# V by Strassen products in a gated cross-attention and FFN block: seven products per pair of key tiles for contexts 1 to 7

## The chip, the cores and the metric

The kernel runs on one core of a Trainium2 chip. The metric is the device time of one execution in microseconds (us), with the span and the granted TensorE clock of the core beside it. In the profile, PE is the TensorE matmul, PEld its weight load, DVE is VectorE, ACT is ScalarE, POOL is GpSimd and SP is SyncE, which here only issues DMAs.

## The reference, cut to what matters

Eight sequences of 1024 rows attend, each with a causal mask, to a context of their own, and a feed-forward network with ternary weights follows. Every product must come out near float32, so the kernel runs each as three float16 passes (see below).

```
x, ctx: (8, 1024, 512); w_q, w_k, w_v: (512, 512); W1: (2048, 512); W2: (512, 2048)

q = layernorm(x) @ w_q;  k = ctx @ w_k;  v = ctx @ w_v
attn = softmax(causal(q @ k.T / sqrt(512)))
x = x + tanh(g_xattn) * (attn @ v)
h = gelu(layernorm(x) @ ternary(W1).T + b1)
x = x + tanh(g_ffn) * (h @ ternary(W2).T + b2)

ternary(w) = clip(round(w / mean|w|), -1, 1)
```

## The kernel before, in words

There are 64 tiles of 128 rows, eight to a context ("batch" in the code). The kernel is written by hand, engine by engine: each engine has its own function `slot`, called once for every tile t, and the order of its lines is the order of that engine's queue. Cross-engine order is by semaphores, and each engine takes its instructions strictly in turn. In what follows, i is t mod 8, the tile's place in its context.

An operand in float32 is split into an upper and a lower float16 half. ACT writes the upper half (`*_upper`), DVE the lower one (`*_lower`), and PE multiplies in three passes (`PASSES`): upper by upper, lower by upper, upper by lower.

In slot t, PE does in this order: the scores of tile t against the (i+1) key tiles of its context, 12 matmuls per 512 keys or rest (L1319); `t_product` for tile t+2, the normalised rows times the product of w_q and w_k, 24 matmuls of 256 columns (L1281); `v_product`, V of key tile t+1, 12 matmuls of 512 columns (L1300); and attn times V of tile t-1, called PV below, 3 matmuls of 512 columns for each key tile up to that tile's own (L1349). Scores of tile t+1 reuse the PSUM of those of tile t.

DVE in slot t: the mask, the row maximum and the bias of the softmax (L909 to L915), statistics of x of tile t+5 (L920), the lower half of the attention weights (L929), `t_lower` (L873), `ln_rows` (L850), `v_lower` (L880), and the output rows of tile t-1 (L956 to L963, "the o update"), which wait for PV. Some slots add a part of the next context: two halves of its maximum (L821), its scale, and `ctx_lower`, the lower half of 256 context columns (L756). In 16 slots a `ternary` step makes 1024 columns of W1 or W2 into -1, 0, 1 (L1091, L1093).

ACT in slot t: the exponential (L573) and the upper half of the weights (L578), `t_upper` (L588), `rows_upper` (L596), `ctx_upper` (L563), `v_upper` (L601). POOL in slot t is short: a power (L446) and the lower half of the normalised rows (L450). SP loads, stores and turns rows by transposing DMAs; it waits in its queue for the o update of every tile before the tile's store (L368).

The raw context of 2 MB lies in `raw`, one context at a time. The float16 weights W1 and W2 lie in `w1_s` and `w2_s`.

The FFN follows. It multiplies the normalised rows by W1 by Strassen's seven products already, in 32 units of 4 hidden tiles (L1198), and then by W2 (`back`, L1254). Its first rows are prepared inside the last attention slots: from tile FIRST_Y = 57 on, each slot normalises one tile (`y_stats`, `y_normal` on DVE), POOL forms sums (`y_sums`, L477 to L482), ACT and POOL split them (`y_upper` L641, `y_lower` L488) and SP turns them (`turn_y`, L334). `weight_sums` (L1004) makes four sums of W1 halves on DVE, two in slot 62 and two in slot 63. PE runs the first three products of unit 0 after the scores of slot 63 (`unit_first`) and goes on after the PV of slot 62 (`unit_second`, which waits for all weight sums).

## Time and profile before

| | us |
|---|---|
| median of 3 runs | 1590.83 (1590.52 to 1591.98) |
| the profiled execution | 1590.56 |
| its span in the trace | 1588.7 |
| granted clock of TensorE, mean | 0.997 |
| PE busy | 1567.5 (99%) |
| DVE busy | 1094.7 (69%) |
| ACT busy | 811.6 (51%) |
| POOL busy | 481.6 (30%) |

A busy PE is the union of modelled matmul intervals, in which the end of one covers the start of the next. How densely PE really works is seen better from the starts in the timeline: a group of n matmuls takes the time to the start of the group behind it. The chain of work that ended last is 95% PE.

### The profile page before, as it was taken

To read this page: it belongs to the slowest core of one execution; us is meant where nothing else is said; L and a number is where in the kernel's file an instruction comes from. 1 tells how busy PE (TensorE), PEld (TensorE's weight loads), DVE (VectorE), ACT (ScalarE), POOL (GpSimd) and SP (SyncE) were. 2 spreads that over 40 slices of the span, in tenths; PEclk is the share of its full clock that TensorE was granted. 3 is DMA by queue.
4 is the path that set the end of the run, shared out by engine and by line. 5 is a ranking of instruction groups with operands and counts; after the bars stand their busy time and mean duration, and the time that the engine had idled before them with its cause. 6 is when DMAs were issued, how large, how long until landed. Compare 5 with 4: busy or idle time off the path is not lost.

```text
span 1588.7 us, 26066 instructions
## 1 busy us (share of the span) xinstructions
PE 1567.5 (99%) x10024; PEld 979.6 (62%) x10024; DVE 1094.7 (69%) x1824; ACT 811.6 (51%) x1448; POOL 481.6 (30%) x468
## 2 busy tenths in 40 slices
PE   7899999999999999999999999999999999999998
PEld 4556555565656565564666666666666666666665
DVE  7766656577787777766567667766776676767654
ACT  2334444433332333333666666666666666666654
POOL 4311111111111111134144444444433453345330
PEclk9999999999999999999999999999999999999999
DMA  8547667654656655553322242233332332324110
GB/s 212 130 103 192 149 182 153 175 137 121 165 128 163 141 160 145 129 123 78 81 77 77 47 100 77 77 67 80 81 87 68 66 98 79 77 47 100 51 51 27
DMA packets 307964, 170.81 MB, mean 108 GB/s; under 512 B 268208, under 2 KB 268224, under 8 KB 306688
## 3 DMA queue, kind: packets, MB, share of 16 engines
q1 hardware_dynamic: 306368, 166.52, 43.0%
q10 hardware_dynamic: 1296, 2.36, 0.4%
q8 instruction: 79, 1.29, 0.3%
q14 instruction: 45, 0.37, 0.1%
q0 software_dynamic: 176, 0.27, 0.1%
HBM read 70.53 MB, written 33.55 MB: 66 GB/s over the span
## 4 chain that ended last, share of the span: by engine, by line
PE 95%; DVE 3%; DMA 1%; issue 1%; ACT 0%; SPq 0%; DVEq 0%
PE s_ps L1254 14%; PE e_ps L1254 14%; PE s_ps L1319 11%; PE o_ps L1349 11%; PE v_ps L1300 10%; PE t_ps L1281 10%; PE t_ps L1198 7%; PE o_ps L1198 7%; PE v_ps L1198 7%; PE m_ps L1198 3%; DMA ctx_s<-in_wqT 1%; DMA raw<-in_ctxT 0%; DVE cmax L821 0%; DVE wv_s L1004 0%; PE e_ps L1349 0%
## 5 line engine op out<-in xcount | busy, mean ns | idle before, releaser
L1056 DVE SCALAR_TENSOR_TENSOR v_s<-xnT,sc,v_s 128x512 f16<-128x512 f32 x256 | 239.0, 954 | 106.3 <-ACT v_s L681 106.3
L674 ACT ACTIVATE xnT<-tT,b_s 128x256 f32<-128x256 f32 x384 | 174.0, 500 | 182.9 <-DVE tT L1050 66.6
L1254 PE MATMUL s_ps<-w_s,v_s 128*128 128x512 f16 x1024 | 262.8, 379 | 0.0
L1254 PE MATMUL e_ps<-w_s,v_s 128*128 128x512 f16 x1024 | 262.8, 379 | 0.0
L573 ACT ACTIVATE p<-s_ps,ebias,esc 128x128 f32<-128x128 f32 (+3 forms) x64 | 53.2, 831 | 339.3 <-DVE ebias L915 339.3
L1319 PE MATMUL s_ps<-ctx_s,tT 128*128 128x512 f16 (+3 forms) x1152 | 197.7, 326 | 3.2 <-DVE tT L873 3.2
L1349 PE MATMUL o_ps<-v_s,pT 128*128 128x512 f16 x840 | 191.6, 379 | 0.1
L681 ACT ACTIVATE v_s<-xnT,sc 128x512 f16<-128x512 f32 x256 | 176.3, 712 | 7.5
L1300 PE MATMUL v_ps<-wv_s,ctx_s 128*128 128x512 f16 x768 | 176.5, 379 | 1.2 <-DVE v_s L880 0.8
L1254 PEld LDWEIGHTS e_ps<-w_s,v_s 128*128 128x128 f16 x1024 | 100.2, 98 | 120.8
L1281 PE MATMUL t_ps<-xnT,a_s 128*128 128x256 f16 x1488 | 172.7, 273 | 0.5 <-ACT a_s L649 0.5
L1319 PEld LDWEIGHTS s_ps<-ctx_s,tT 128*128 128x128 f16 x1152 | 105.8, 98 | 95.1 <-DVE tT L873 4.1
L1281 PEld LDWEIGHTS t_ps<-xnT,a_s 128*128 128x128 f16 x1488 | 144.8, 98 | 22.8 <-issue 0.9
L501 POOL TENSOR_TENSOR tT<-tT 128x512 f32<-128x512 f32 x64 | 81.5, 1273 | 245.7 <-ACT tT L701 245.7
L446 POOL TENSOR_TENSOR rstd<-var_s,minus_half 128x1 f32<-128x1 f32 x61 | 34.0, 557 | 382.8 <-DVE var_s L844 382.8
L1349 PEld LDWEIGHTS o_ps<-v_s,pT 128*128 128x128 f16 x840 | 82.1, 98 | 97.2 <-DMA pT<-p_s 0.6
L1254 PEld LDWEIGHTS s_ps<-w_s,v_s 128*128 128x128 f16 x1024 | 100.2, 98 | 67.1
L1300 PEld LDWEIGHTS v_ps<-wv_s,ctx_s 128*128 128x128 f16 x768 | 74.9, 98 | 78.9 <-issue 1.0
L450 POOL TENSOR_TENSOR xn_both<-xn_both 128x512 f16<-128x512 f32 x61 | 70.9, 1162 | 165.0 <-ACT xn_both L596 165.0
L1038 DVE COPY tT<-t_ps 128x512 f32<-128x512 f32 x64 | 44.3, 692 | 92.8 <-PE t_ps L1198 92.8
L471 POOL TENSOR_TENSOR rstd<-var_s,minus_half 128x1 f32<-128x1 f32 x64 | 35.1, 548 | 226.9 <-DVE var_s L1016 226.9
L880 DVE SCALAR_TENSOR_TENSOR v_s<-v_ps,v_s 128x512 f16<-128x512 f32 x64 | 44.1, 689 | 74.9 <-ACT v_s L601 74.9
(176 smaller groups left out, 2411.9 us busy)
## 6 DMA issues: line engine op xcount, KB each, us to landing
out_y<-x_ring SPq DMA_DIRECT2D x128, 256.0 KB, 2.2
x_ring<-in_x SPq DMA_DIRECT2D x63, 256.0 KB, 2.9
raw<-in_ctxT SPq DMA_DIRECT2D x7, 2048.0 KB, 7.9
raw<-out_y SPq DMA_DIRECT2D x44, 256.0 KB, 3.7
w_in<-in_w1T SPq DMA_DIRECT2D x16, 512.0 KB, 3.9
w_in<-in_w2T SPq DMA_DIRECT2D x16, 512.0 KB, 3.9
x_ring<-out_y SPq DMA_DIRECT2D x20, 256.0 KB, 3.5
xnT<-xn_both SPq DMA_TRANSPOSE x128, 2.7
```

Source lines behind the costliest of these rows:

```text
L450: g.tensor_tensor(xn_s[:, r, LO], xn32[:, r], xn_s[:, r, HI], ALU.subtract).then_inc(xn_lo, 1)
L501: g.tensor_tensor(rr[:, R3], rr[:, R3], rr[:, R5], ALU.add).then_inc(c22_sum, 1)
L573: a.activation(p32[:, 0:w], s_ps[:, 0:w], ACT.Exp, bias=ebias[:, r:r + 1], scale=esc[:, (s // TB) % 2:(s // TB) % 2 + 1], accum_out=rowsum ...
L674: a.activation(g32n[:, j, half * 2 * P:(half + 1) * 2 * P], src, ACT.Gelu, bias=b1_s[:, f:f + 1], scale=1.0 / YN).then_inc(g_act, 1)
L681: a.activation(g_s[:, U % 2, j, HI], g32n[:, j], ACT.Copy, scale=col(C_SG)).then_inc(g_hi, 1)
L1056: v.scalar_tensor_tensor(out=g_s[:, U % 2, j, LO], in0=g32n[:, j], scalar=col(C_SG), in1=g_s[:, U % 2, j, HI], op0=ALU.mult, op1=ALU.subtr ...
L1198: last_mm = mm(bank[:, p * 2 * P:(p + 1) * 2 * P], w, yT[g % 2][:, a, row, c, :], start=(first and p == 0 and a == HI and c == 0), stop=(a ...
L1254: last_mm = mm(y_ps[i], g_s[:, U % 2, j, a, i * P:(i + 1) * P], w2_s[:, f, :], start=(U % UG == 0 and n == 0 and a == HI), stop=(U % UG == ...
L1281: last_mm = mm(bank[:, dd], a_s[:, aa, c, d * P:(d + 1) * P], xnT[:, pr, xa, c, :], start=(n == 0 and c == 0), stop=(n == 2 and c == DC - 1))
L1300: last_mm = mm(v_ps[:, :], ctx_s[:, par, ca, c, j * P:(j + 1) * P], wv_s[:, va, c, :], start=(n == 0 and c == 0), stop=(n == 2 and c == DC ...
L1319: last_mm = mm(s_ps[:, lo:hi], tT[:, pr, ta, c, q * P:(q + 1) * P], ctx_s[:, par, ca, c, lo:hi], start=(n == 0 and c == 0), stop=(n == 2 a ...
L1349: last_mm = mm(o_bank(last, s), pT[:, (s - 1) % 2, pa, j], v_s[:, par, va, j], start=(n == 0 and j == 0), stop=(n == 2 and j == jn))
```

## The change

V of context 0 stays as it was. For contexts 1 to 7 the eight `v_product`s of a context become four pairs (28 pairs u in all). A pair is two key tiles (256 rows) by 512 inputs by 512 outputs, cut in two each way, and is computed by Strassen's seven products, each of 3 passes by 2 matmuls of 256 columns: 42 matmuls of 256 columns where there were 24 of 512.

Four sums of raw context blocks are formed on POOL (`ctx_parts`, once a pair) and split by ACT and DVE (`ctx_parts_upper`, `ctx_parts_lower`, 1024 columns each); four sums of w_v are formed once (`weight_parts`). The products are spread over three slots: one and two in slot 5+2u (`v_pre`), six, five, seven and three in slot 6+2u, four in slot 7+2u. Product six stands ahead of the scores of its slot and waits for `ctx_parts_lower` of the slot before. ACT copies three partial results out of PSUM, DVE adds three times and splits the four blocks of V in three instructions. V is made about a context ahead of its use.

The context is laid out and loaded in quarters. One quarter is split in every even slot; its maximum is taken quarter by quarter in odd slots. For the first quarter of a context, `ctx_scale`, `ctx_upper` and `ctx_lower` stand in the same slot (i = 4).

W2 in float16 takes over `raw`. A ternary step is now two comparisons and a subtraction. Ternary steps stand in 13 slots (29 to 31, 37 to 39, 45, 46, 53 to 56, 60), and the last three are made on DVE in FFN units 0 to 2, loaded into `p32`. FIRST_Y moves from 57 to 58; `y_upper` and `y_lower` of the third row pair move into FFN unit 0; `weight_sums` move a slot earlier, to slots 61 and 62. The scale of V's operands is 2^11 rather than 2^13.

```diff
-        w2_s = sb("w2_s", [P, FC, D], F16)
-        WR = 3
+        v_work = sb("v_work", [P, 8192], F16)
+        vr = sb("vr", [P, 3, D // 2])
+        WR = 2
+        w2_s = raw[:, :].bitcast(F16).rearrange("p (f d) -> p f d", d=D)
+        NP = (NT - TB) // 2
+        SPLIT_AT, PRE_AT, MAIN_AT, LAST_AT = 4, 5, 6, 7
+        def pair(t, at):
+            u, odd = divmod(t - at, 2)
+            return u if not odd and 0 <= u < NP else None
+                  **{t: "T" for t in (29, 30, 31, 37, 38, 39, 45, 46, 53, 54, 55, 56, 60)}}
-        FIRST_Y = NT - 7
+        FIRST_Y = NT - 6
...
+            def ctx_parts(u):
...
+                pool.wait_ge(ctx_in[q], ctx_landed(b, q))
+                pool.wait_ge(sums_split, u)
+                g.tensor_tensor(sums32[:, 0], a21, a22, ALU.add).then_inc(sums_made, 1)
+                g.tensor_tensor(sums32[:, 2], a11, a21, ALU.subtract).then_inc(sums_made, 1)
+                pool.wait_ge(sums_made, 4 * u + 1)
+                g.tensor_tensor(sums32[:, 1], sums32[:, 0], a11, ALU.subtract).then_inc(sums_made, 1)
+                pool.wait_ge(sums_made, 4 * u + 3)
+                g.tensor_tensor(sums32[:, 3], a12, sums32[:, 1], ALU.subtract).then_inc(sums_made, 1)
...
+                if pair(t, SPLIT_AT) is not None:
+                    ctx_parts(pair(t, SPLIT_AT))
                 if not last or t + LN_LEAD < NT:
                     norm(it, s)
...
                     rows_upper(it, s)
-                if not last or t + 1 < NT:
+                if t + 1 < TB:
                     v_upper(it, s)
+                if pre is not None:
+                    v_first(pre)
+                if tail is not None:
+                    v21_upper(tail)
+                if main is not None:
+                    v12_upper(main)
+                    vd_upper(main)
+                if split is not None:
+                    ctx_upper(b, par, q)
...
                 if norm:
                     ln_rows(k, rk, src, s + LN_LEAD >= 2)
-                for m, n in terns[:1]:
-                    ternary(m, n)
-                if not last or t + 1 < NT:
+                if pre is not None:
+                    ctx_parts_lower(pre)
+                if tail is not None:
+                    v21(tail)
+                if pre is not None:
+                    v11(pre)
+                if tail is not None:
+                    v21_lower(tail)
+                if main is not None:
+                    v22(main)
+                    v12_lower(main)
+                    vd_lower(main)
+                if t + 1 < TB:
                     v_lower(it, s)
-                if last and t == NT - 2:
+                if last and t == NT - 3:
                     weight_sums(0)
                     weight_sums(1)
-                if last and t == NT - 1:
+                if last and t == NT - 2:
                     weight_sums(2)
                     weight_sums(3)
...
-                v.scalar_tensor_tensor(out=w_dst(n), in0=w_in[:, m % WR], scalar=col(th), in1=w_neg[:, :],
-                                       op0=ALU.is_gt, op1=ALU.subtract).then_inc(w_ternary, 1)
+                v.tensor_scalar(w_dst(n), src, col(th), None, ALU.is_gt).then_inc(w_negs, 1)
+                dve.wait_ge(w_negs, 2 * n + 2)
+                v.tensor_tensor(w_dst(n), w_dst(n), w_neg[:, :], ALU.subtract).then_inc(w_ternary, 1)
...
+            def v_six(u):
+                pe.wait_ge(vr_out, nth_of(u, 1))
+                pe.wait_ge(sums_split, u + 1)
+                v_part(u, 6)
...
+                if main is not None:
+                    v_six(main)
                 if not last or t < NT:
...
+                if main is not None:
+                    v_five(main)
                 if s > 0 and (not last or t < NT - T_LEAD):
                     t_product(it, s)
+                if main is not None:
+                    v_seven_three(main)
+                if tail is not None:
+                    v_four(tail)
+                if pre is not None:
+                    v_pre(pre)
```

PE, from slot i = 1 of a middle context into slot i = 2. Before, from `t_product` on; behind the last row come the scores of slot i = 2.

```order
L1281 MATMUL t_ps<-xnT,a_s 128x256 [waits t_split,x_turned1,x_turned0]
L1281 MATMUL t_ps<-xnT,a_s 128x256 x23
L1300 MATMUL v_ps<-wv_s,ctx_s 128x512 [waits v_split,ctx_split]
L1300 MATMUL v_ps<-wv_s,ctx_s 128x512 x11
L1349 MATMUL o_ps<-v_s,pT 128x512 [waits o_done,v_split,p_turned0]
L1349 MATMUL o_ps<-v_s,pT 128x512 x2
```

And now, from product four on; the last row but two is product six of the next slot.

```order
L1566 MATMUL e_ps<-v_work,ctx_s 128x256 [waits vb_sum]
L1566 MATMUL e_ps<-v_work,ctx_s 128x256 x5
L1566 MATMUL e_ps<-wv_s,ctx_s 128x256 [waits vb_split,ctx_split]
L1566 MATMUL e_ps<-wv_s,ctx_s 128x256 x5
L1566 MATMUL v_ps<-wv_s,ctx_s 128x256 [waits vb_sum]
L1566 MATMUL v_ps<-wv_s,ctx_s 128x256 x5
L1709 MATMUL o_ps<-v_s,pT 128x512 [waits vb_split,o_done,p_turned0]
L1709 MATMUL o_ps<-v_s,pT 128x512 x2
L1566 MATMUL e_ps<-v_work 128x256 [waits sums_split,vr_out]
L1566 MATMUL e_ps<-v_work 128x256 x5
L1664 MATMUL s_ps<-ctx_s,tT 128x384 [waits p_exp,ctx_split,t_split]
```

The first matmul behind the PV no longer is the scores but product six, which waits for `sums_split`, DVE's `ctx_parts_lower` of the slot before.

DVE in the same slot (i = 1), from the lower half of the attention weights to the o update. Before:

```order
L929 SCALAR_TENSOR_TENSOR p_s<-p,p_s 128x256 [waits p_hi]
L873 SCALAR_TENSOR_TENSOR tT<-t_ps,tT 128x512 [waits t_hi]
L850 TENSOR_SCALAR xn_both<-x_ring,mv,rstd 128x512 [waits xn_lo,ln_rstd]
L880 SCALAR_TENSOR_TENSOR v_s<-v_ps,v_s 128x512 [waits v_hi]
L956 RECIPROCAL rinv<-rowsum 128x1
```

And now:

```order
L1183 SCALAR_TENSOR_TENSOR p_s<-p,p_s 128x256 [waits p_hi]
L1126 SCALAR_TENSOR_TENSOR tT<-t_ps,tT 128x512 [waits t_hi]
L1103 TENSOR_SCALAR xn_both<-x_ring,mv,rstd 128x512 [waits xn_lo,ln_rstd]
L1031 SCALAR_TENSOR_TENSOR v_work<-v_work,csc 128x1024 [waits sums_hi]
L1052 TENSOR_TENSOR vr<-vr,e_ps 128x256 [waits vr_out,vp4_mm]
L1040 TENSOR_TENSOR vr<-vr,v_ps 128x256 [waits vr_out,vp2_mm]
L1074 SCALAR_TENSOR_TENSOR v_s<-vr,v_s 128x256 [waits vb_hi]
L1222 RECIPROCAL rinv<-rowsum 128x1
```

`ctx_parts_lower` (`v_work<-v_work,csc`) stands behind `ln_rows`, and three more instructions on V stand ahead of the o update.

SP in slots 62 and 63, now: the turn of the second row pair (`ctx_s<-v_s`) stands behind the store of tile 61, which waits for that tile's o update; before it stood a slot earlier, ahead of the turn of tile 62's weights.

```order
L420 DMA_TRANSPOSE pT<-p_s 128x7x128 [waits p_split,pv_mm]
L420 DMA_TRANSPOSE pT<-p_s 128x7x128
L453 DMA out_y<-x_ring 128x512 [waits o_done]
L410 DMA_TRANSPOSE ctx_s<-v_s 128x28x128 [waits y_lo]
L420 DMA_TRANSPOSE pT<-p_s 128x8x128 [waits p_split,pv_mm]
```

Product one of FFN unit 0 on PE still waits for both turns (`y_turned0`, `y_turned1`).

## Rows read from the trace of the kernel before

**Rows 1.** Attention without its start: us, busy PE, PEld, DVE, ACT, POOL; clock, DMA.

```profile
75.90:719.70 643.80, 643.80 (x3945) 379.20 (x3946) 455.29 (x907) 236.22 (x409) 108.20 (x126) 1.00 0.61 147
```

**Rows 2.** Timeline of PE, slots 41 and 42: start, us, engine, line, operation.

```profile
493.86 1.47 PE L1319 MATMUL s_ps<-ctx_s,tT 128*128 128x256 f16 x12
495.17 2.78 PE L1281 MATMUL t_ps<-xnT,a_s 128*128 128x256 f16 x24
497.79 2.75 PE L1300 MATMUL v_ps<-wv_s,ctx_s 128*128 128x512 f16 x12
500.38 0.81 PE L1349 MATMUL o_ps<-v_s,pT 128*128 128x512 f16 x3
501.02 2.11 PE L1319 MATMUL s_ps<-ctx_s,tT 128*128 128x384 f16 x12
```

**Rows 3.** Timeline of DVE and ACT in slot 41, where the attention weights are narrow.

```profile
495.70 0.42 DVE L911 TENSOR_REDUCE negmax<-s_ps 128x1 f32<-128x256 f32 x1
497.99 0.60 ACT L588 ACTIVATE tT<-t_ps 128x512 f16<-128x512 f32 x1 [0.47 <-PE t_ps L1281]
498.62 0.69 DVE L873 SCALAR_TENSOR_TENSOR tT<-t_ps,tT 128x512 f16<-128x512 f32 x1 [0.65 <-ACT tT L588]
499.22 0.54 DVE L850 TENSOR_SCALAR xn_both<-x_ring,mv,rstd 128x512 f32<-128x512 f32 x1
499.80 0.63 ACT L596 ACTIVATE xn_both<-xn_both 128x512 f16<-128x512 f32 x1 [1.21 <-DVE xn_both L850]
```

**Rows 4.** Groups by line: the operations nearest to the added ones (mean ns).

```profile
L756 DVE SCALAR_TENSOR_TENSOR ctx_s<-raw,csc,ctx_s 128x1024 f16<-128x1024 f32 x32 | 40.3, 1277 | 0.0
L480 POOL TENSOR_TENSOR v_s<-v_s 128x256 f32<-128x256 f32 x17 | 12.3, 724 | 0.0
L1091 DVE TENSOR_SCALAR g<-w_in,sc 128x1024 f16<-128x1024 f32 x16 | 12.0, 748 | 0.1
L1093 DVE SCALAR_TENSOR_TENSOR w_s<-w_in,sc,g 128x1024 f16<-128x1024 f32 x16 | 36.0, 2253 | 0.6
```

**Rows 5.** Timeline in slot 43 (i = 3): the mask, and the upper half of the weights.

```profile
514.85 0.29 DVE L909 TENSOR_TENSOR s_ps<-s_ps,causal 128x128 f32<-128x128 f32 x1
517.06 0.63 ACT L578 ACTIVATE p_s<-p 128x512 f16<-128x512 f32 x1
```

**Rows 6.** Timeline in FFN: a DVE instruction beside one of POOL, and two beside four.

```profile
819.04 1.27 POOL L501 TENSOR_TENSOR tT<-tT 128x512 f32<-128x512 f32 x1 [1.01 <-ACT tT L701]
819.54 1.32 DVE L1056 SCALAR_TENSOR_TENSOR v_s<-xnT,sc,v_s 128x512 f16<-128x512 f32 x1 [0.35 <-ACT v_s L681]
833.29 7.63 POOL L495 TENSOR_TENSOR x_ring<-x_ring,b_row 128x512 f32<-128x512 f32 x4
838.88 2.59 DVE L1056 SCALAR_TENSOR_TENSOR v_s<-xnT,sc,v_s 128x512 f16<-128x512 f32 x2
```

**Rows 7.** Timeline of the passage to FFN, slots 62 and 63.

```profile
719.85 4.70 PE L1319 MATMUL s_ps<-ctx_s,tT 128*128 128x512 f16 x24
720.80 2.14 DVE L1030 TENSOR_SCALAR w_in<-raw,mv,rstd 128x512 f32<-128x512 f32 x1
722.68 4.24 SPq L334 DMA_TRANSPOSE ctx_s<-v_s  x1
727.52 0.95 ACT L578 ACTIVATE p_s<-p 128x896 f16<-128x896 f32 x1
...
742.13 3.58 POOL L488 TENSOR_TENSOR xn_both<-w_in,xn_both 128x1792 f16<-128x1792 f32 x1 [2.54 <-ACT xn_both L641]
742.24 4.62 DVE L1004 TENSOR_TENSOR wv_s<-w_s 128x1024 f16<-128x1024 f16 x2
748.13 1.89 PE L1198 MATMUL t_ps<-ctx_s,wv_s 128*128 128x256 f16 x8 [3.89 <-DVE wv_s L1004]
```

**Rows 8.** The page: `y_upper` of a row pair; the landing of its turn.

```profile
L641 ACT ACTIVATE v_s<-v_s 128x1792 f16<-128x1792 f32 x17 | 28.8, 1696 | 27.7 <-POOL v_s L482 27.7
ctx_s<-v_s SPq DMA_TRANSPOSE x17, 6.1
```

More of the change, by code:

```diff
@@ L369, in slot @@
                 if t == 1:
-                    load_ctx(1)
-                if s % TB == 7 and (not last or t + 9 < NT):
-                    load_ctx(it * 2 + s // TB + 2)
+                    for q in range(NQ):
+                        load_ctx(1, q)
             for i in range(8):
                 sp.sem_inc(x2_stored[i], 16)
-            for i in range(4):
-                sp.sem_inc(y_stored[i], 16)
             for r in range(2):
@@ L1330, in slot @@
                     unit_first(0)
-                if not last or t + 1 < NT:
+                if t + 1 < TB:
                     v_product(it, s)
```

402 lines of the change are left out of this document (317 added, 85 removed).

## The prediction, made before the changed kernel was run

> **What bounds the kernel now.** I read the page first: PE is busy for 99% of the span, the chain that ended last is 95% PE, the granted clock is 0.997. Then the stages. Between 75.9 and 719.7 us PE never shows a gap, while DVE is busy for 455.3 of 643.8 us, 71%, ACT for 37% and POOL for 17% [rows 1]. A busy PE may still wait, so I looked at starts. From 493.86 to 501.02 us every group follows the one before without a gap: 24 matmuls of 256 columns take 495.17 to 497.79, 0.1092 us each; 12 of 512 columns take 497.79 to 500.38, 0.2158 us each [rows 2]. PE is the bound there, and work taken from it is gained one for one as long as nobody else is late. The exception is the passage to FFN, where PE waits 3.89 us for `weight_sums` [rows 7].
>
> **What Strassen takes from PE.** A pair cost 24 x 0.2158 = 5.18 us and will cost 42 x 0.1092 = 4.59 us. The difference is 0.59 us, for 28 pairs 16.6 us. That matmuls of 256 columns keep this pace with a weight load for each is seen in `t_product`, which is of this form [rows 2]. Start from the profiled execution: 1590.6 - 16.6 = 1574.0, if nothing else moves.
>
> **What it gives to DVE, ACT and POOL.** For each pair DVE loses two `v_lower`, 0.69 us each like `t_lower` [rows 3], and gains `ctx_parts_lower`, as wide as `ctx_lower`, 1.28 us [rows 4], one split of 512 elements (0.69) and five operations of 256, each about 0.42 by the reduction of that width [rows 3]. That is 4.07 - 1.38 = +2.7 us a pair, 75 us in all. The 13 ternary steps get shorter: 0.75 + 2.25 us before; now 0.75 + 0.75 and a float16 subtraction of 0.68 (what a weight sum takes unhindered; bounds 0.5 to 1.3), -0.8 each. DVE goes from 71% to about 83% of the stage. On average it fits; the question is when each result comes, because slots differ: 6.5 us of PE at i = 1, 14.3 at i = 7.
>
> **Product six waits at i = 2.** It is PE's first work in the even slot and needs `ctx_parts_lower` of the slot before. With the new products PE's slot i = 1 is 1.31 (scores) + 2.62 + 0.66 (four) + 1.31 (one, two) + 0.65 (PV) = 6.54 us. The chain cannot be that short: `t_product` ends 3.93 us after the slot's start, `t_upper` starts 0.20 later, then `t_lower` and `ln_rows` run until 499.76, 5.90 after the start [rows 3]; `ctx_parts_lower` adds 1.28, the release some 0.07. Six can start at 7.25, 0.7 late. DVE also comes late into this slot: behind the o update, which ends about 0.95 after the PV, stands `ctx_lower` (1.2), so its mask starts at 2.15 rather than 1.51. That makes 0.8 us. It happens in 7 contexts: **+5.6**.
>
> **Again at i = 4.** In slot i = 2 the new work stands behind `rows_upper` on ACT: from `t_product`'s end (5.9) on, `t_upper` 0.6, `t_lower` 0.6, `ln_rows` 0.55, `rows_upper` 0.65, the upper half of one block 0.4, of the diagonal 0.6, its lower half 0.6, two small operations 0.45, the o update 0.7 and `ctx_lower` 1.2, one behind the other. DVE is free 12.4 us after the slot's start, and the slot lasts 8.5 on PE. So DVE masks tile i = 3 at 3.9 where its scores are there at 2.8. From the mask it takes 2.2 to the upper half, which takes 0.63 [rows 5], then `t_upper` 0.6, `t_lower` 0.6, `ln_rows` 0.54, `ctx_parts_lower` 1.28: 9.85, against 9.1 of PE. Six waits 0.75 us, in 6 contexts (the last has no rows left to normalise): **+4.8**, bounds 1 and 8. At i = 6 the same sum comes out even (11.6 against 11.7), though the new scale, `ctx_upper` and `ctx_lower` of i = 4 run one behind the other; I take 0, at most 3.
>
> **Ternary steps beside POOL.** `ctx_parts` is four POOL operations of 0.72 us [rows 4], and begins when POOL has finished the rows of the odd slot before, 12.7 us into slot i = 5 and about 13 into i = 7. DVE then is at its ternary step. In this trace a DVE instruction with two operands in SBUF and one of POOL do not run together: the 0.71 us split of 819.54 took 1.32 and ended 0.55 after POOL's; two of them beside four POOL operations took 2.59 instead of 1.41, and POOL's four 7.63 instead of 5.3 [rows 6]. `y_normal`, a TENSOR_SCALAR as the comparisons are, took 2.14 instead of 0.54 us, to the end of a POOL instruction whose result SP turned from 722.68 on [rows 7]. They take turns. A step of 2.2 us then takes up to 4.2. DVE carries the delay along: by my walk through slots 29 to 33, it enters i = 0 5.5 to 8.1 us late, where the slot absorbs 5.0; the rest arrives at the short slot i = 1 and is added to the wait there. That gives 0.5 to 4.3 us in each of two contexts, under 1 where only slots 45 and 46 have steps, and 2.6 to 6.4 in the context with steps up to slot 56 (i = 0). Bounds 3.7 and 16; I take **+7**. The Trainium skill, "SBUF — State Buffer", section "Who interferes with whom", says that a DVE instruction with two SBUF inputs, or in a 2-port mode, and a GpSimd instruction that reads SBUF hold a shared pair of ports for a whole instruction, whoever comes first. By that rule all three instructions of a step and all four of `ctx_parts` queue for one another and the term is at its upper end, 16; were it a mere sharing of bandwidth, each would stretch a little and the term be near 3.7. The trace agrees with the rule (1.32 against 0.71 us, and it ends 0.55 after POOL's).
>
> **The passage to FFN.** The 3.89 us for `weight_sums` and the low clock behind it (eight matmuls of 256 columns are busy for 1.89 us [rows 7], and the two groups take 1.4 us more than 16 x 0.109) go away: -5.3 us. But the second row pair is now made in slot 62, which has no V work left and lasts only 4.54 + 3.89 = 8.4 us on PE. From its start (before: 719.85): softmax done at 8.6 [rows 7]; `y_upper` 1.7 [rows 8] until 10.3; POOL's `y_lower` 3.6 until 13.9 [rows 7]; the turn lands 6.1 later [rows 8], at 20.0 at the earliest. The third and fourth weight sums run on DVE just then; beside `y_lower` a pair of them took 4.62 instead of 1.3 [rows 7]. The o update of tile 61 stands behind them, and SP stores that tile ahead of the turn. So 22 to 23.4 is likelier. PE wants the turned rows after the scores of slot 63, at 8.4 + 5.2 = 13.6, and waits 8.4 to 9.8 us, with about 1.5 for the clock again. Net: 9.1 + 1.5 - 5.3 = 5.3, rounded to **+5**, bounds +1 (turn at 20.0, no clock lost) and +7.
>
> **At no cost.** The three late ternary steps: DVE and POOL have gaps of 2 us and more in every FFN unit, and `back` of unit 3 comes 13 us later than the load; the third pair's `y_lower` delays lower halves that have over 5 us. If that cover is gone, 1 to 3 us. `weight_parts` on POOL and ACT in slots 3 and 4, and the fuller slots 5 to 7: +0.5, bounds 0 and 3. The loads by quarters move the same bytes. SP's `load_ctx` waits for `ctx_lower` ahead of the turn of the weights, which wait longer for `p_split`.
>
> **Sum.** 1590.6 - 16.6 + 5.6 + 4.8 + 7 + 5 + 0.5 = 1596.9; the median lies 0.3 above the profiled execution. I forecast **1597 us**.
>
> **Rivals.** (1) *DVE stays in time, faster*: six waits only at i = 2, ternary and POOL hardly meet, the passage costs +3. 1590.8 - 16.6 + 5.6 + 3 + 1 = 1583.8. For it speaks that DVE has 17% left over and that all long slots absorb delay; against it, that the short ones do not. (2) *About even*: as forecast, but the ternary steps cost 3.7 and the passage 4: 1592.8. (3) *The turns of POOL and DVE cost most, far slower*: steps at 16 and six also late at i = 6 (3), the passage at 7: 1590.8 - 16.6 + 5.6 + 4.8 + 16 + 3 + 7 = 1610.6. It decides from a delay of DVE of 5 us at the start of a context; below that nothing arrives. (4) *The products do not deliver*: if the small products did not run at 0.109 us, each 0.01 us more would cost 1176 x 0.01 = 11.8 us. Against it stand 1488 matmuls of this form at that pace.
>
> **Chances.** Forecast 0.42, rival 1 0.20, rival 2 0.18, rival 3 with 4 0.20. The forecast and rivals 3 and 4 are slower by over 0.2% (above 1594.0), rival 2 lies within 0.2%, rival 1 is faster by more (below 1587.6); 0.2% is about what a measurement of this kernel can tell from no change. So faster 0.20, same 0.18, slower 0.62. The range reaches from 1584 (rival 1) to 1607.
>
> **What would show each step.** Six's wait for DVE's split at L1031: about 0.8 us in slots 10, 18, ... 58, and 0.75 in 12, 20, ... 52; in slots 34 and 42 2 to 4 us, in 58 more. PE's groups of product at 0.109 us a matmul, 4.6 us a pair. The ternary instructions in slots 29, 37, 45 and 53 drawn out beside POOL's operations of `ctx_parts`. One wait of 8 to 10 us for a turn at product one of unit 0, none for weight sums. FFN as long as before from unit 1 on. I am wrong if six starts right behind PV in the short slots, since then 10 us of my sum are gone, or if the turn lands before PE has done the scores of slot 63.

## The result and the profile after

| | before | changed |
| --- | --- | --- |
| median, us | 1591.4 (4 runs, 1590.5 to 1592.1) | 1607.9 (4 runs, 1605.8 to 1609.8) |
| ratio, 95% interval | | 1.0105 [1.0092, 1.0118] |
| profiled execution, us (span) | 1590.6 (1588.7) | 1606.55 (1604.7) |
| PE busy, us (share) | 1568 (99%) | 1559.4 (97%) |
| granted clock | 0.997 | 0.994 |

The changed kernel is 1.05% slower: 16.5 us. The forecast of 1597 us had the direction right and less than half of the size; 1607.9 lies just above the end of its range, 1607.

The page of the changed kernel: busy time of the engines, with shares of the span and instructions:

```profile
PE 1559.4 (97%) x10528; PEld 1027.8 (64%) x10528; DVE 1178.0 (73%) x1996; ACT 878.5 (55%) x1589; POOL 592.5 (37%) x585
```

The waits of PE in the changed kernel (operation and line <- what ended the wait: us in total, times, longest):

```profile
PE e_ps L1566 <- DVE v_work L1031: 12.5, 14, 2.1
PE v_ps L1470 <- issue: 6.9, 1, 6.9
PE m_ps L1537 <- DVE g L1083: 4.0, 1, 4.0
PE o_ps L1709 <- DMA pT<-p_s: 3.9, 1, 3.9
PE s_ps L1664 <- DVE tT L1126: 3.3, 3, 1.9
PE e_ps L1566 <- DVE ctx_s L945: 2.1, 1, 2.1
```

The third and most of the fifth are in the start of the kernel, where the kernel before waits too (4.0 and 3.2 us). The others are new: product six for `ctx_parts_lower` (L1031), product one of FFN, the P V product of tile 61, and product one of the first pair for `ctx_lower` (L945). By windows of the stages (us, busy PE, PEld, DVE, ACT, POOL, granted clock, DMA, GB/s), the changed kernel:

```profile
151.00:720.00 569.00, 555.61 (x3942) 377.47 (x3940) 466.47 (x946) 267.60 (x491) 183.83 (x207) 1.00 0.59 144
720.00:800.00 80.00, 66.61 (x397) 39.38 (x396) 54.02 (x84) 35.57 (x60) 30.92 (x26) 0.94 0.45 108
```

In the first stage PE of the kernel before has no gap [rows 1]; here it is without work for 13.4 us. DVE is at 82% (466.47 of 569.00), as forecast (83%).

The timeline of PE at the end of slot 59 (i = 3), where product six of slot 60 stands, and in the passage (start, us, engine, line, operation, idle time before it):

```profile
704.19 0.81 PE L1566 MATMUL e_ps<-v_work 128*128 128x256 f16 x6 [0.71 <-DVE v_work L1031]
...
726.70 4.71 PE L1664 MATMUL s_ps<-ctx_s,tT 128*128 128x512 f16 x24 [0.84 <-DVE tT L1126]
735.30 4.06 PE L1709 MATMUL o_ps<-v_s,pT 128*128 128x512 f16 x18 [3.88 <-DMA pT<-p_s]
739.19 5.34 PE L1664 MATMUL s_ps<-ctx_s,tT 128*128 128x512 f16 x24
751.48 1.86 PE L1470 MATMUL v_ps<-ctx_s,w_s 128*128 128x256 f16 x8 [6.95 <-issue]
753.14 1.91 PE L1470 MATMUL t_ps<-ctx_s,wv_s 128*128 128x256 f16 x8
```

The 16.6 us of Strassen are there: from start to start, the groups of small products follow each other at 0.109 us a matmul where nothing is waited for. What ate them can be added up from the starts of PE's groups. For each group I took the time to the next group's start less its matmuls at the pace of [rows 2] (0.1092 us for 256 columns, 0.2158 for 512):

| where | forecast | in the trace |
| --- | --- | --- |
| product six, i = 2, without ternary steps | +5.6 | 7 x 0.73 = +5.1 |
| the same, longer in three contexts (1.96, 1.73 and 2.22 us) | +7 | +3.7 |
| product six, i = 4 | +4.8 | 0.73 to 0.88, seven times: +6.0 |
| product six, i = 6 | 0 | 6 x 0.27 = +1.6 |
| start, up to the scores of slot 6 | +0.5 | 104.54 - 99.52 us, less 1.97 for the new products: +3.1 |
| passage to FFN, net, from the PV of tile 60 to that of tile 63 | +5 | 15.0 - 5.5 = +9.5 |
| first FFN units | 0 | 0.81 + 1.19 + 0.22 + 0.99, or +3.2 |

1590.6 - 16.6 + 32.2 = 1606.2 us, against 1606.55 measured in the profiled execution; the kernel's median lies 1.4 us above that. Product six as a whole came out near the forecast (16.4 us against 17.4; at i = 4 it waits in the last context too). The miss is in the last three rows: 10.3 us. The 15.0 us of the passage are 12.2 us at its three waits and 2.8 us of slow matmuls behind the last one; the forecast had 9.1 and 1.5.

### The profile page after: what moved, and what is told of

Same layout as the page of the kernel before. It is cut to its first block, busy times and chain, and to the rows that moved or that the text cites. A ratio compares the mean times of both kernels' runs of the same rounds, so it can differ in the third digit from the quotient of the medians.

```text
span 1604.7 us, 27825 instructions
## 1 busy us (share of the span) xinstructions
PE 1559.4 (97%) x10528; PEld 1027.8 (64%) x10528; DVE 1178.0 (73%) x1996; ACT 878.5 (55%) x1589; POOL 592.5 (37%) x585
## 4 chain that ended last, share of the span: by engine, by line
PE 74%; DVE 15%; issue 5%; ACT 4%; DMA 1%; SPq 1%; POOL 0%; DVEq 0%; ACTq 0%
PE s_ps L1528 13%; PE e_ps L1528 13%; PE t_ps L1470 7%; PE v_ps L1470 7%; PE o_ps L1470 7%; PE s_ps L1664 7%; PE o_ps L1709 6%; PE t_ps L1623 5%; PE e_ps L1566 4%; PE m_ps L1470 3%; DVE ctx_s L945 2%; DVE negmax L1165 1%; DVE v_work L1031 1%; DVE x_ring L1229 1%; DVE xn_both L1103 1%
## 5 line engine op out<-in xcount | busy, mean ns | idle before, releaser
L1528 PE MATMUL s_ps<-raw,v_s 128*128 128x512 f16 x1024 | 262.8, 379 | 0.8 <-DVE raw L1364 0.8
L1528 PE MATMUL e_ps<-raw,v_s 128*128 128x512 f16 x1024 | 262.8, 379 | 0.0
L1528 PEld LDWEIGHTS e_ps<-raw,v_s 128*128 128x128 f16 x1024 | 100.2, 98 | 120.8
L1528 PEld LDWEIGHTS s_ps<-raw,v_s 128*128 128x128 f16 x1024 | 100.1, 98 | 68.1 <-issue 1.1
L539 POOL TENSOR_TENSOR xn_both<-xn_both 128x512 f16<-128x512 f32 x61 | 79.1, 1297 | 166.7 <-ACT xn_both L770 166.7
L770 ACT ACTIVATE xn_both<-xn_both 128x512 f16<-128x512 f32 x64 | 40.4, 632 | 92.7 <-DVE xn_both L1103 89.9
L1566 PE MATMUL e_ps<-v_work 128*128 128x256 f16 x504 | 68.7, 272 | 13.4 <-DVE v_work L1031 12.5
L1314 DVE TENSOR_TENSOR tT<-tT,t_ps 128x512 f32<-128x512 f32 x64 | 44.1, 688 | 51.2 <-ACT tT L884 28.1
```

The costliest lines, as they stand in the source:

```text
L539: g.tensor_tensor(xn_s[:, r, LO], xn32[:, r], xn_s[:, r, HI], ALU.subtract).then_inc(xn_lo, 1)
L1528: last_mm = mm(y_ps[i], g_s[:, U % 2, j, a, i * P:(i + 1) * P], w2_s[:, f, :], start=(U % UG == 0 and n == 0 and a == HI), stop=(U % UG == ...
L1566: last_mm = mm(bank, left(ca, c), right(va, c), start=(first and n == 0 and c == 0), stop=(n == 2 and c == 1), skip_group_check=True)
```

## The experiments

Each edit starts from the changed kernel. "-" is the changed kernel's line, "+" the experiment's. Medians are of four runs unless said otherwise.

### Product six behind the scores

```diff
  # PE, slot
- v_six(main); scores; v_five(main); t_product(it, s)
+ scores; v_six(main); t_product(it, s); v_five(main)
  # ACT, slot
- v_second(main); v_third(main); softmax(it, s); t_upper(it, s)
+ v_second(main); softmax(it, s); t_upper(it, s); v_third(main)
```

> The changed kernel with product six moved behind the scores of its slot (it stood ahead of them), product five behind the T product, and ScalarE's copies moved to match (the copy after six ahead of the softmax, the copy after five behind the T remainder's upper half). The theory: VectorE delivers ctx_parts_lower 0.7 to 2.2 us too late for the first instruction of the slot and would be in time for one that stands 1.3 us (12 score matmuls at i=0) or more later, so 8.8 us at i=2, 6.0 us at i=4 and 1.6 us at i=6 go: 1607.9 - 16.4 = 1591.5. Rival A: VectorE as a whole is behind, and the scores then wait for t_lower, which stands one 1.27 us instruction ahead of ctx_parts_lower: only waits up to 1.3 us go, the three long ones (1.96, 1.73, 2.22) leave 0.7 each: 1594. Rival B: ScalarE's copies, now behind the softmax, come late for product three in every pair, 0.3 us or more in 28 pairs: 1600 or above, with waits for ACT vr in the trace.

Measured: 1618.8 us, 10.9 slower than the changed kernel. Its waits of PE:

```profile
PE e_ps L1567 <- ACT vr L719: 20.0, 13, 3.0
```

No wait for `v_work` (`ctx_parts_lower`) is left, and none for the T remainder took its place, so rival A is out: DVE does deliver within the time of the scores. But 20.0 us of waits for ACT's copy of product five came in its place (rival B, though I had sized it at 0.3 us in 28 pairs, 8.4 us). The edit put that copy behind the softmax and `t_upper`; in the changed kernel it stands ahead of them. The edit moved two things, and the second cost more than the first gave. The waits alone make a loss of 3.6 us (20.0 against 16.4). The trace has another 6.4 us in groups of matmuls behind the longest of them, where the granted clock was lower: 0.79 from 474 to 482 us, for example.

### ctx_parts_lower earlier on DVE, alone and with ACT's copy

```diff
  # DVE, slot
+ if pre is not None: ctx_parts_lower(pre)
  dve.wait_ge(p_hi, t + 1)   # the p remainder
  ...
  ln_rows(...)
- if pre is not None: ctx_parts_lower(pre)
```

> The changed kernel with one instruction moved on VectorE: ctx_parts_lower (1.27 us) of the odd slot stands ahead of the p remainder (in the idle time before it of about 0.8 us) and no longer behind the T remainder and the row normalization. Nothing is moved on TensorE. The theory: the copy that it needs has long been made on ScalarE, only its place in VectorE's order made product six wait; the waits of 8.8 us at i=2, 6.0 us at i=4 and 1.6 us at i=6 go: 1607.9 - 16.4 = 1591.5. Rival A: the p remainder and the T remainder come 0.5 us later and scores or P V products of small i wait for them: 0.5 us in 28 pairs goes back, 1605 at i of 2 alone (7 x 0.5), 1595. Rival B: the three long waits at i=2 (1.96, 1.73, 2.22) come from VectorE being behind as a whole, and turn into waits for t_lower of 1 us each: 1594.5.

Measured: 1612.9 us, 5.0 slower than the changed kernel. That is none of the three outcomes that I had written down. The waits:

```profile
PE e_ps L1566 <- ACT vr L707: 15.2, 13, 2.2
```

Product six waits for two things: DVE's lower part and ACT's copy of product one (`v_first`, L707). The copy stands on ACT behind `rows_upper`, and that waits for DVE's `ln_rows`. With `ctx_parts_lower` ahead of it, `ln_rows` comes later, and the copy with it: by 0.8 us in slot 33, counted from `t_upper` (part of the 1.28 us fills idle time of DVE). In slot 33 of this run, ACT:

```profile
418.72 0.58 ACT L762 ACTIVATE tT<-t_ps 128x512 f16<-128x512 f32 x1
421.30 0.63 ACT L770 ACTIVATE xn_both<-xn_both 128x512 f16<-128x512 f32 x1 [2.00 <-DVE xn_both L1103]
421.83 0.37 ACT L707 ACTIVATE vr<-e_ps 128x256 f32<-128x256 f32 x1
```

ACT idled 2.00 us, up to 421.30, with product one finished at 418.6. Behind the two longest waits of product six the next matmuls are slow as well, by 1.7 us each time. So I moved the copy ahead of that wait as well:

```diff
  # ACT, slot
  t_upper(it, s)
+ if pre: v_first(pre)
  rows_upper(it, s)
- if pre: v_first(pre)
```

> As the run lower (ctx_parts_lower ahead of the p remainder), and on ScalarE the copy of product one (v_first) ahead of rows_upper, which waits for VectorE's row normalization. In the run lower the waits of product six for v_work were gone and waits for the copy of product one stood in their place, 15.2 us in 13 waits. The theory: product six waits for two deliveries; the copy stood behind rows_upper and so behind VectorE too. With both moved, product one ends 1.3 us after the T product and its copy 0.5 us later, ahead of the end of the P V product for every i, and the waits go: 1612.9 - 15 = 1598 by the run lower, 1607.9 - 16.4 = 1591.5 by the changed kernel. Rival: the two deliveries are not the end of it; scores or P V wait for t_lower, x rows or the p transposes next, since VectorE is behind as a whole in the odd slots: above 1600.

Measured: 1599.6 us, 8.3 faster than the changed kernel, 13.3 faster than with DVE's half of the edit alone. DVE's half alone loses; with ACT's half it gains. In the changed kernel both deliveries had come late, 0.26 us apart, and the profile names the later one; for the same slot 33, DVE and ACT:

```profile
417.48 1.28 DVE L1031 SCALAR_TENSOR_TENSOR v_work<-v_work,csc 128x1024 f16<-128x1024 f32 x1
```

```profile
418.13 0.37 ACT L707 ACTIVATE vr<-e_ps 128x256 f32<-128x256 f32 x1
```

Half of the 16.4 us came back. Most of the rest is here:

```profile
PE e_ps L1568 <- ACT vr L714: 5.4, 6, 1.2
```

L714 is the copy of product six, on which product five waits. The copy itself waits for the lower half of the last block of the pair before (L1076), which now runs beside POOL's lower half of the rows (L539); in slot 33 of this run, POOL, DVE and ACT:

```profile
415.55 1.15 POOL L539 TENSOR_TENSOR xn_both<-xn_both 128x512 f16<-128x512 f32 x1 [1.72 <-ACT xn_both L770]
415.81 1.17 DVE L1076 SCALAR_TENSOR_TENSOR v_s<-vr,v_s 128x256 f16<-128x256 f32 x1 [0.34 <-ACT v_s L738]
...
417.07 0.38 ACT L714 ACTIVATE vr<-e_ps 128x256 f32<-128x256 f32 x1 [1.30 <-DVE v_s L1076]
```

This split takes 1.17 us in 26 of the 28 pairs of this run and 0.42 in the other two; in the changed kernel its median was 0.48. So the edit has a price of its own: the new order makes DVE meet POOL once more in nearly every pair. In contexts 1 to 3 only 0.2 to 0.3 us a context is left. In contexts 4 to 7, which have the ternary steps, DVE also reaches the split later (1.4 us behind the start of the scores of slot 34, against 0.5 in slot 10), and there the waits of 0.6 to 1.2 us stand. This is what the rival meant by DVE being late as a whole.

### The ternary step in its old form

```diff
  # DVE, ternary step
- tensor_scalar(w_dst, src, th, is_gt); tensor_tensor(w_dst, w_dst, w_neg, subtract)
+ scalar_tensor_tensor(w_dst, src, th, w_neg, is_gt, subtract)
```

> The changed kernel with the ternary step in the form of before: comparison (2x), then one SCALAR_TENSOR_TENSOR from the float32 source (about 1.3 us) in place of comparison (0.75) and 2-byte subtraction (0.68 alone, 3.95 beside POOL). The theory: the form matters only where the subtraction meets POOL, at slot 60 (3.95 us) and at the first FFN units, about 1.0 us in front of the scores and some of the 3.0 us at the FFN start; elsewhere the two forms cost 1.4 and 1.3 us: 1607.9 - 3 = 1605. Rival: the three contexts whose product six waited 1.0 to 1.5 us more owe it to this form: a further 3.7 us, 1601.

Measured: 1603.9 us, 4.0 faster. The three long waits of product six at i = 2 fell from 1.96, 1.73 and 2.22 us over nominal to 1.13, 0.73 and 1.54, its waits in all from 12.5 to 9.9 us, and the scores of tile 62 no longer waited 0.84. Both the theory and its rival hold in part. The passage is 1.7 us shorter in this trace, but the first FFN units, where the theory saw a gain, lose 4.1 us in place of 3.2. How a step and POOL's four operations of `ctx_parts` share their time is seen at 400 us in the changed kernel (the step of slot 31 and the sums of slot 32); first DVE, then POOL:

```profile
400.01 1.21 DVE L1361 TENSOR_SCALAR g<-w_in,sc 128x1024 f16<-128x1024 f32 x1
401.14 1.21 DVE L1362 TENSOR_SCALAR w_s<-w_in,sc 128x1024 f16<-128x1024 f32 x1
402.39 1.10 DVE L1364 TENSOR_TENSOR w_s<-w_s,g 128x1024 f16<-128x1024 f16 x1
```

```profile
400.64 1.17 POOL L561 TENSOR_TENSOR v_work<-raw 128x256 f32<-128x256 f32 x1
401.77 1.17 POOL L563 TENSOR_TENSOR v_work<-v_work,raw 128x256 f32<-128x256 f32 x1
```

They alternate, and each instruction is longer by 0.4 to 0.5 us: the three of a step take 3.5 us from start to end where they take 2.1 alone. The step costs 1.4 us more, not the 2.0 of my walk. A step with two instructions meets POOL's turn twice and not three times: the same step in this run takes 2.9 us. In the changed kernel the subtraction takes between 0.69 and 3.95 us.

The prediction counted a step of the new form 0.8 us shorter than one of the old; that came from a row read wrongly. L1093 takes 2.25 us on average in the kernel before [rows 4], but there it ran beside POOL's lower half of the rows; the same instruction takes 1.28 us in this run where POOL is idle (second fence):

```profile
363.66 2.28 DVE L1093 SCALAR_TENSOR_TENSOR w_s<-w_in,sc,g 128x1024 f16<-128x1024 f32 x1
363.70 1.16 POOL L450 TENSOR_TENSOR xn_both<-xn_both 128x512 f16<-128x512 f32 x1 [3.15 <-ACT xn_both L596]
```

```profile
389.50 1.28 DVE L1363 SCALAR_TENSOR_TENSOR w_s<-w_in,sc,g 128x1024 f16<-128x1024 f32 x1
```

So alone the old form takes 2.0 us and the new one 2.1: the step did not get 0.8 us shorter.

### The start: two edits

```diff
  # PE, slot 5
- v_pre(0); v_product(0, 5)
+ v_product(0, 5); v_pre(0)
  # DVE: v11(0) behind v_lower
```

> The changed kernel with the products one and two of the first pair (v_pre(0), slot 5) moved behind the V product of that slot, and VectorE's v11(0) behind v_lower. The theory: the 2.28 us in which TensorE waited at 94.9 us for ctx_lower (chain of ctx_scale, ctx_upper, ctx_lower, after weight_parts_lower) are filled by a V product of 2.6 us, and with the wait goes part of the lower clock of the next 5 us (1.19 and 0.49 us over nominal): 1607.9 - 2.3 to 4.0 = 1604.8. Rival: the wait moves, to v_product for VectorE or to product six for the copy of product one: 1607.4.

Measured: 1608.8 us, no gain, as the rival had it. The wait for `ctx_lower` was filled and came back at product six, for a delivery that I had not named:

```profile
PE e_ps L1568 <- DVE v_work L1023: 3.4, 1, 3.4
```

It waits for the second half of the weight parts' remainder, which took 2.17 us at 101.08 beside POOL. With the weight parts' upper halves at the end of slot 3 and both remainders in slot 4:

```diff
  # ACT
- slot 4: weight_parts_upper() ahead of v_upper
+ slot 3: weight_parts_upper() behind v_upper
  # DVE
- slot 4: weight_parts_lower(0); slot 5: weight_parts_lower(1)
+ slot 4: weight_parts_lower(0); weight_parts_lower(1)
```

> As the run start (products one and two of the first pair behind the V product), and the weight parts earlier: ScalarE's upper halves at the end of slot 3 in place of slot 4, both of VectorE's remainders in slot 4 in place of slots 4 and 5. In the run start, product six waited 3.4 us for the second remainder (2.17 us at 101.08). The theory: that wait was the only one that the move opened, so the 2.28 us at 94.9 and what the clock lost behind it go: 1604.5. Rival: the copy of product one or v11, now behind the V product, come late for six (0.8 us or more), or the wait for ctx_lower stays in front of the V product: 1607.

Measured: 1606.8 us, the rival's number. It is 1.1 below the changed kernel, but the ranges (1605.0 to 1607.0, and 1605.8 to 1609.8) overlap, so a gain is not shown. In its trace the 2.28 us at the T product of slot 5 are gone, and 1.46 us stand in front of product six, for the copy of product one: the rival took a good half of it.

### The passage to FFN

The SP queue of the changed kernel, and POOL and DVE, between the y rows and product one (on SP the time is that of the issue):

```profile
723.49 5.68 SPq L410 DMA_TRANSPOSE ctx_s<-v_s  x1
729.35 2.54 SPq L420 DMA_TRANSPOSE pT<-p_s  x2
...
744.77 0.35 SPq L453 DMA_DIRECT2D out_y<-x_ring  x1
745.16 4.47 SPq L410 DMA_TRANSPOSE ctx_s<-v_s  x1
```

```profile
715.67 3.82 POOL L607 TENSOR_TENSOR v_s<-v_s 128x1792 f16<-128x1792 f32 x1 [4.32 <-ACT v_s L830]
...
737.30 4.11 POOL L607 TENSOR_TENSOR v_s<-v_s 128x1792 f16<-128x1792 f32 x1 [1.97 <-ACT v_s L830]
```

```profile
716.09 3.95 DVE L1364 TENSOR_TENSOR raw<-raw,g 128x1024 f16<-128x1024 f16 x1
...
737.89 5.75 DVE L1268 TENSOR_TENSOR a_s<-w_s,wv_s 128x1024 f16<-128x1024 f16 x2
```

The p transposes of tile 61 (729.35) stand behind the first y transpose; the second one (745.16) stands behind a store that waits for the o update, and that behind the weight sums. The first edit touched the queue alone:

```diff
  # SP
- turn_y(0) ahead of turn_p in slot 61; turn_y(1) ahead of turn_p in slot 63
+ turn_y(0) behind turn_p in slot 61; turn_y(1) behind turn_p, ahead of the store, in slot 62
```

> The changed kernel with two transposes of y rows moved on the SP queue: that of pair 0 behind the p transposes of slot 61 (ahead of them before), that of pair 1 to slot 62, behind its p transposes and ahead of the store of tile 61 (slot 63 before). The theory: the P V product of tile 61 waited 3.88 us because its p transposes stood behind the first y transpose (5.68 us of issue), and product one of FFN waited 6.95 us of which 3.7 us because the second y transpose stood behind a store that waits for the o update at 743.99, itself behind weight_sums. Both go: 1607.9 - 3.9 - 3.7 = 1600.3. Rival: POOL's y_lower (4.11 us, end 741.4) and the o update tie what comes before, the gain of the first wait only lets the scores end earlier and lengthens the second wait: only 3.7 us in all, 1604.2.

Measured: 1605.0 us, 3.0 faster, near the rival's 1604.2. The 3.88 us at the P V product went, and the wait of product one grew from 6.9 to 7.4 us: counted from the scores of tile 62, PE was ready for it 3.8 us sooner and the rows were there 3.3 us sooner. They could have been there earlier still but for this:

```profile
739.32 1.70 ACT L830 ACTIVATE v_s<-v_s 128x1792 f16<-128x1792 f32 x1 [0.93 <-DMA ctx_s<-v_s]
```

`y_upper` of the second row pair writes the buffer that the first transpose reads. In the changed kernel the rows of the second pair are one chain of about 20 us, from `y_normal` at 731.31 on: four operations on POOL, `y_upper`, `y_lower` (4 us), nearly 4 us until the transpose is issued, and 6 until it has landed. That this chain sets the time, and not the wait ahead of it, is seen in the runs whose edits left the passage alone: the wait of the P V product and that of product one were 3.9 and 6.9 us in the changed kernel, 1.6 and 9.2 in the run with product six moved, 1.7 and 9.2 in the first run on the start, 1.7 and 9.1 in the run with both copies moved. They add up to 10.8 or 10.9 us each time; only in the second run on the start was it less, 3.5 and 5.7. The next edit shortened the chain itself:

```diff
- POOL, slots 60 and 62: y_lower(0), y_lower(1)
+ DVE, slot 60: y_lower(0); slot 62: y_lower(1), ahead of weight_sums(2) and (3)
- SP: as above
+ SP: turn_y(0) and turn_y(1) behind turn_p and ahead of the store in slots 60 and 62
```

> The changed kernel with y_lower of pairs 0 and 1 on VectorE (slots 60 and 62, there ahead of weight_sums) in place of POOL, and both y transposes on the SP queue at the end of slots 60 and 62, behind the p transposes and ahead of the store. The theory: the chain of y rows is what the passage waits for (7.4 us left in the run with the transposes moved alone, since y_upper of pair 1 waited for the transpose of pair 0 and y_lower took 3.66 us on POOL). y_lower on VectorE takes about 1.9 us, the 2-byte weight sums no longer meet it (4.67 to 5.75 us for two against 1.28), and the transpose of pair 1 issues at about 740 in place of 745: product one waits 1.5 us in place of 6.95 and the P V product of tile 61 at most 1 us in place of 3.88: 1607.9 - 5.4 - 2.9 = 1599.6. Rival: y_lower on VectorE delays the p or o work of its slot, and the transposes of 4.3 to 5.7 us delay the p transposes of the next slot: no more than the 3.0 us of the run before is gained, 1605.

Measured: 1599.0 us, 8.9 faster (forecast 8.3). On DVE the two `y_lower` and the weight sums behind them, and what PE still waits for:

```profile
716.43 2.02 DVE L1327 TENSOR_TENSOR v_s<-v_s 128x1792 f16<-128x1792 f32 x1
...
735.84 3.08 DVE L1327 TENSOR_TENSOR v_s<-v_s 128x1792 f16<-128x1792 f32 x1
738.85 1.28 DVE L1268 TENSOR_TENSOR a_s<-w_s 128x1024 f16<-128x1024 f16 x2
740.05 1.28 DVE L1268 TENSOR_TENSOR a_s<-w_s,wv_s 128x1024 f16<-128x1024 f16 x2
```

```profile
732.19 4.06 PE L1709 MATMUL o_ps<-v_s,pT 128*128 128x512 f16 x18 [2.07 <-DMA pT<-p_s]
745.12 1.87 PE L1470 MATMUL v_ps<-ctx_s,w_s 128*128 128x256 f16 x8 [3.69 <-issue]
```

The weight sums take 1.28 us a pair again and not 5.75, and product one starts 6.4 us sooner. The edit moved `y_lower` and the transposes at once; what each is worth alone is not shown beyond the 3.0 us of the run before.

### The late ternary steps

```diff
- "T" at slot 60, and three steps in FFN units 0 to 2, their sources loaded into p32
+ "T" at slots 57, 59, 60, 61; none in FFN
```

> The changed kernel with all four late ternary steps in attention (slots 57, 59, 60, 61; in the changed kernel one in slot 60 and three in FFN units 0 to 2, whose sources are loaded into p). The theory: the FFN start loses 3.0 us to them (excess of 0.81, 1.19, 0.22 and 0.99 us over the nominal pace between 787 and 815 us), and slots 59 to 61 have VectorE time for them, since product six stands there no more: 1607.9 - 3 = 1605. Rival: steps of 2.2 us in slots 60 and 61, one of which meets POOL's y_lower (3.95 us for the subtraction), put the y rows later, which the passage waits for: 1610.

Measured: 1609.2 us against 1607.9, within the range of the changed kernel (1605.8 to 1609.8): no gain, and a loss is not shown; the rival had 1610. The excess in the first FFN units fell from 3.2 to 1.6 us, so the steps caused half of it (the rest is in front of products that wait 1.3 us for one copy of ACT, L878 there). Three other places gave more back, by the trace: product six of slot 60 waited 2.4 us in place of 0.7, the pair's product one 0.5 us for `ctx_lower`, and the passage became 1.2 us longer. In the passage:

```profile
719.15 3.95 DVE L1358 TENSOR_TENSOR raw<-raw,g 128x1024 f16<-128x1024 f16 x1
...
742.99 5.73 DVE L1262 TENSOR_TENSOR a_s<-w_s,wv_s 128x1024 f16<-128x1024 f16 x2
```

Product one then waited 10.7 us in place of 6.9, the P V product 2.2 in place of 3.9.

### Put together

The first sum: `ctx_parts_lower` early (without ACT's half), the passage, the start's second form, the ternary step in the old form, and that of slot 60 in slot 57.

> All of it together: ctx_parts_lower ahead of the p remainder, y_lower on VectorE with the transposes moved, the start with the weight parts earlier, the ternary step in the form of before, and its step of slot 60 in slot 57. The theory (the changed kernel's loss is a sum of separate waits): 1607.9 - 16.4 (six) - 8.3 (passage) - 3.4 (start) - 1 (ternary) = 1579, faster than before by 12 us, of the 16.6 us that the products save. Rival: VectorE is the bound once the waits are gone from one place, and they come back at another: above 1588.

Measured: 1597.1 us (8 runs), 10.8 faster than the changed kernel and 18 above what I expected. The sum had counted 16.4 us for the edit to DVE's order, which loses alone, and it shows the same waits: 14.6 us for ACT's `v_first`, in 15 waits. With that copy moved, the late steps in attention, and product one of FFN unit 0 behind the P V product of tile 62:

```diff
  # PE, slot 63
- unit_first(0); P V of tile 62
+ P V of tile 62; unit_first(0)
  # ACT, DVE, slot 63
- unit_copy(0); softmax / the p remainder
+ softmax / the p remainder; unit_copy(0)
```

> All moves together: those of all1, v_first ahead of rows_upper, the late ternary steps in attention (form of before), and product one of FFN unit 0 behind the P V product of tile 62 with the copies and softmax of slot 63 in that order. The theory: all1 (1597.1) had left 14.6 us of waits for the copy of product one, 4.4 us for the y transpose, and 3.5 us over nominal at the FFN start; they go for 14 + 3.5 + 2.5: 1577. Rival: VectorE, busy 73%, is then late for something else in each pair (0.3 us in 28 pairs) and the late steps lengthen the passage: 1588.

Measured: 1588.25 us (11 runs), ratio to the kernel before 0.9981 [0.9972, 0.9990]. The rival's number, by its second half: the passage, where the late steps now stand.

```profile
PE o_ps L1708 <- DVE x_ring L1228: 4.8, 2, 3.0
```

No wait for a y transpose is left; 4.8 us are P V products that wait for DVE's o update, 3.0 of them behind the ternary step of slot 61 and two weight sums, 1.7 behind `y_lower` (3.08 us there) and the other weight sums. The last run moved the step of slot 61 to slot 58.

> As the run all3, with the last four ternary steps in slots 57 to 60 in place of 57, 59, 60 and 61. The theory: in all3 the step of slot 61 (0.75 + 1.28 us, and 0.82 us of waiting for its data) put VectorE's o update of tile 60 to 722.52 us, and the P V product of tile 61 waited 3.02 us for it; slot 58 has room. That wait falls to about 1 us (what all1 had for the p transposes): 1588.25 - 2 = 1586.3. Rival: the last p transposes or the y rows come no sooner, and the passage gives the wait back behind the scores of tile 62: 1588.2.

Measured: 1587.5 us (8 runs) against 1591.7 for the kernel before, measured beside it, ratio 0.9974 [0.9963, 0.9984]. That lies between the theory's 1586.3 and the rival's 1588.2, and does not tell them apart. The 4.8 us fell to 2.2, but the step in slot 58 now holds up `ctx_lower`:

```profile
PE e_ps L1565 <- DVE ctx_s L939: 3.1, 2, 2.8
PE o_ps L1708 <- DVE x_ring L1228: 2.2, 1, 2.2
```

So the change, with its work placed otherwise, is faster than the kernel before by 0.26%, or 4.2 us, where the products save 16.6. Not tested is what the same edits of the passage (`y_lower` on DVE, the transposes ahead of the stores) would give the kernel before, which loses 5.5 us there; so the 4.2 us are the difference of two kernels and not the worth of the products. A difference between the last two versions is not shown, since their ranges overlap (1587.3 to 1590.0, and 1585.1 to 1588.8).

## Why the prediction was half right

The steps that failed are three terms of the sum: the passage (+5, measured +9.5), the start (+0.5, measured +3.1) and the late ternary steps "at no cost" (0, measured +3.2). The mechanism was right in the main; these terms were mis-sized, each for a reason of its own.

- **What bounds the kernel; Strassen's saving.** Right. PE is the bound, the small products keep 0.109 us, and where the waits were taken away the time came down with them.
- **Product six at i = 2 and i = 4.** Right in place and size: 0.73 and 0.86 us against 0.8 and 0.75. At i = 6 I had taken 0 of "at most 3"; it was 1.6. My mechanism was incomplete, though: I had one chain, over DVE. There is a second, over `ln_rows`, `rows_upper` and ACT's `v_first`, that ends close to the first; my expectation gave a full gain for moving `ctx_parts_lower`, and it cost 5 us.
- **Ternary steps beside POOL.** I took +7 of 3.7 to 16, and the lower bound was right. They do take turns, in single instructions. I over-counted how often they meet, and a meeting costs a step 1.4 us, not 2.0. Undoing the form alone gives 4.0 us, some of it in the passage. That the form is the cause of all 3.7 us is not shown: 1.2 of them are left with the old form. One reading of the prediction was wrong: "-0.8 each" for the steps. The 2.25 us of the old form held a turn of POOL already; alone it takes 1.28, and the new form saved nothing.
- **Product six in all.** 16.4 us against 17.4 is luck in part: 3.3 too much for the ternary steps and 0.5 at i = 2 cancel 1.2 too little at i = 4 and 1.6 at i = 6.
- **The start.** This step failed: "+0.5, bounds 0 and 3", measured +3.1. I had costed the operations of `weight_parts` and not their place in the chain ctx_scale, ctx_upper, ctx_lower, on which product one of the first pair waits. The trace has 2.28 us at that product and 1.7 of slow matmuls behind it, less what the slots ahead were shorter by. The edits show it as two chains again: take away one wait and the other is 1.5 to 3.4 us behind it.
- **The passage.** The step that failed by most: "+5, bounds +1 and +7", measured +9.5. The chain of the second row pair was longer than forecast: product one started 24.8 us after slot 62 did, not 22 to 23.4. Its own wait was 6.95 us and not 8.4 to 9.8, because 3.88 us had been lost before it: SP issued the first y transpose ahead of tile 61's p transposes. I had walked through SP's queue for the second pair and not for the first. On top came 0.84 us at the scores of tile 62, which wait behind the late ternary step of slot 60, and 2.8 us of slow matmuls where I had taken 1.5. The edits on queue and `y_lower` gave 8.9 us back, so the chain of queue and `y_lower` is shown to be the cause.
- **"At no cost": the late ternary steps.** I named the price if the cover is gone, 1 to 3 us, and took 0 on the ground of gaps of 2 us per unit; the first FFN units lost 3.2. The run without the steps in FFN shows 1.6 us for them there. The remaining 1.6 go with the third pair's rows, by the trace only: `y_upper` keeps ACT for 1.70 us from 789.92 on, ahead of the copy (L884, at 792.32) that a product of the unit waits for.

The rivals: the first (DVE in time) fell with the waits of product six. The second had the ternary term right (3.7) and the passage wrong (4). The fourth fell with the 0.109 us. The third ended near the truth by number, 1610.6, for a wrong reason: its 16 us for the turns of POOL and DVE are not there. The upper end of the range, 1607, lay 10 us above the sum; by their own bounds the three terms that failed had 7.5 us of room, and together they were 10.3 us out.

## What to carry to other kernels

When work is added to a filled pipeline, an instruction has as many chains behind it as it has waits; cost each of them, since the profile names only the one that ended last, and a move of one may be worth less than nothing until the other is moved (here +5.0 us alone, -8.3 with the other). Before a long mean is taken as an instruction's cost, look at what runs beside it. Pass every queue once for each thing that is moved, and not for the last one only. And cost "at no cost" edits in the short, dense stretches (a start, a passage between stages) as carefully as the steady state: here the steady state came out within 1 us of the forecast, in part by errors that cancel, and the rest of the miss lay in some 100 us around it.
